# A ViT tower kernel: the decay column goes through device memory, block copies go to GpSimd, and several banks change hands

## The reference

```python
q, k = l2norm(silu(conv(x Wq))), l2norm(silu(conv(x Wk)));  v = silu(conv(x Wv))
alpha, beta = sigmoid(x Wa), sigmoid(x Wb)
def step(St, inp):                       # a scan over the 3137 tokens
    Sk = St @ kt
    Sn = a * (St - b * Sk[:, None] * kt[None, :]) + b * vt[:, None] * kt[None, :]
    return Sn, Sn @ qt
out = linear(zc_rmsnorm(gdn) * silu(x Wg), Wo)
```

## Time and profile before

| | |
|---|---|
| median of 3 runs | 950.95 us (950.13 to 955.2) |
| the profiled execution: time, span | 952.8 us, 951.1 us |
| PE busy | 866.4 us (91%) |
| DVE busy | 672.8 us (71%) |
| ACT busy | 515.1 us (54%) |
| POOL busy | 323.4 us (34%) |
| DMA | 42.52 MB, mean 45 GB/s |

### The profile page before, as it was taken

How to read it: one execution, slowest core, us unless ns; L and a number is a source line. 1 busy time by engine, 2 the same in 40 slices (tenths; PEclk the granted TensorE clock), 3 DMA queues, 4 the chain that set the end, 5 groups by cost and what they waited for, 6 DMA issues and landing times. The chain is left out here.

```text
span 951.1 us, 31438 instructions
## 1 busy us (share of the span) xinstructions
PE 866.4 (91%) x11991; PEld 656.8 (69%) x11991; DVE 672.8 (71%) x2445; ACT 515.1 (54%) x1846; POOL 323.4 (34%) x430
## 2 busy tenths in 40 slices
PE   4799999999999999999999999999977699999996
PEld 2467777777777777777776777777666477777675
DVE  4466778777778777777878777777773486777534
ACT  0445555556655565665555565655543346566664
POOL 3112222122222212222222222222210048889875
PEclk9989999999999999999999999999996699999999
DMA  2000111111111000000000000000000214334341
GB/s 53 6 7 7 51 40 51 40 51 46 30 51 41 29 21 26 28 26 29 29 18 29 18 29 26 28 29 13 24 25 12 89 45 122 112 106 128 101 117 56
DMA packets 60160, 42.52 MB, mean 45 GB/s; under 512 B 3233, under 2 KB 52579, under 8 KB 60012
## 3 DMA queue, kind: packets, MB, share of 16 engines
q1 hardware_dynamic: 59163, 39.98, 14.0%
q10 hardware_dynamic: 848, 0.54, 0.2%
HBM read 20.97 MB, written 19.53 MB: 43 GB/s over the span
## 5 line engine op out<-in xcount | busy, mean ns | idle before, releaser
L408 ACT ACTIVATE logit<-bank 128x2 f32<-128x2 f32 x100 | 17.4, 174 | 161.0 <-PE bank L1010 161.0
L1009 PE MATMUL bank<-SA,work 128*128 128x386 f32 x200 | 94.9, 558 | 3.5 <-ACT work L511 2.9
L1500 ACT ACTIVATE work<-bank,b1mix 128x512 f32<-128x512 f32 x96 | 66.0, 687 | 58.2 <-PE bank L1592 58.1
L1618 PEld LDWEIGHTS bank<-work 128*128 128x128 f32 x768 | 89.5, 192 | 11.5 <-issue 11.5
L1618 PE MATMUL bank<-work 128*128 128x128 f32 x768 | 89.6, 275 | 0.0
L1592 PE MATMUL bank<-work 128*128 128x512 f32 x192 | 86.5, 593 | 0.0
L592 POOL TENSOR_TENSOR expo<-euler,logit 128x8 f32<-128x8 f32 x25 | 40.9, 1638 | 133.0 <-ACT logit L408 133.0
L1010 PE MATMUL bank<-SB,work 128*128 128x256 f32 x200 | 61.2, 388 | 0.0
L612 POOL TENSOR_TENSOR oscale<-ovar,half_neg 128x4 f32<-128x4 f32 x25 | 25.2, 1008 | 105.3 <-DVE ovar L854 105.3
L716 DVE TENSOR_TENSOR work<-bank,work 128x128 f32<-128x128 f32 x100 | 29.2, 292 | 44.5 <-PE bank L997 42.7
L1010 PEld LDWEIGHTS bank<-SB,work 128*128 128x128 f32 x200 | 39.5, 197 | 28.6 <-issue 3.1
(11 more groups left out here) (239 smaller groups left out, 2339.9 us busy)
## 6 DMA issues: line engine op xcount, KB each, us to landing
hn_kept<-work SPq DMA_DIRECT2D x25, 256.0 KB, 2.3
hnT_kept<-work SPq DMA_DIRECT2D x25, 256.0 KB, 2.3
work<-hnT_kept SPq DMA_DIRECT2D x25, 256.0 KB, 3.1
work<-hn_kept SPq DMA_DIRECT2D x25, 256.0 KB, 3.3
out_dram<-work SPq DMA_DIRECT2D x24, 256.0 KB, 2.5
tv<-in_L_ffn_tv_W_dram SPq DMA_DIRECT2D x16, 256.0 KB
work<-in_x_dram SPq DMA_DIRECT2D x23, 102.0 KB
work<-in_projections_dram ACTq DMA_DIRECT2D x1, 257.0 KB
```

What stands on the lines that cost most here:

```text
L1009: mm(t[:, 0:386], xs[p][:, b, HIST:XW], SA[:, 0:386], start=True, stop=False)
L1500: ins = nc.scalar.activation(hid[f][:, :], ps[:, :], ACT.Relu, bias=b1mix[:, of[0], f:f + 1])
L1618: ins = mm(by4(bank[2 + par])[:, t, :], hid[f][:, t * C:(t + 1) * C], w2T[of[t]][:, f, :], start=(f == 0 and t == 0), stop=(f == FB - 1), ...
```

## The change

Seven edits. (1) `g`: row 0 of `decay` and `glast` now lie in one tile `decay_g`; SP writes that row to device memory and, when it has landed, reads it back as a column (128x4 single elements) and as a broadcast row. The five small PE operations go. (2) The six copies of `Xd` and `Yd` blocks move from ACT to POOL. (3) `level_blocks(6)` writes bank 7 and no longer waits for `X`'s level-5 blocks, only for `Y`'s. (4) The transposed `rmat` goes to bank 2 and stands before `level_blocks(6)` on PE; it waits for the decay scan. (5) `og` is transposed into bank 7, and `wo` moves into the next iteration, behind `km`. (6) POOL computes `expo` after `rmat`. (7) DVE takes the E statistics one level earlier, and `expo1`, `ab` and `kd` before `new_blocks(4)`; on ACT the relu comes after the copies of `X`'s last block and `ogT`.

```diff
@@ SP, at the end of an iteration
+                if on(j, LF):
+                    s = j + LF
+                    sp.wait_ge(glast_ready, s + 1)
+                    sp.dma_start(g_dram[s:s + 1, :], decay_g[0:1, :]).then_inc(g_out, 16)
+                    sp.wait_ge(g_out, 16 * (s + 1))
+                    need(sp, gs_ready, s - 1)
+                    need(sp, state_ready, s - 1)
+                    sp.dma_start(g_raw[s % 2][:, 0:NB], g_dram[s, 0:NB * C].rearrange("(b t) -> t b", b=NB), ...).then_inc(g_in[s % 2], 16)
+                    sp.dma_start(g_raw[s % 2][:, NB:3 * NB], g_dram[s, NB * C:NB * C + 2 * NB].partition_broadcast(D)).then_inc(g_in[s % 2], 16)
@@ ACT
-                    act.wait_ge(Y_ready, 5 * (s + 1))
-                    for r in (0, 1):
-                        nc.scalar.copy(Y[sub(r), :, sub(r)], Yd[par][sub(r)])
-                    for r in (2, 3, 0, 1):
-                        nc.scalar.copy(X[par][sub(r), :, sub(r)], Xd[par][sub(r)])
...
-                (the relu of gf, L488 to L495)
...
-                    nc.scalar.copy(ogT, by4(bank[5])).then_inc(ogT_ready, 1)
+                    nc.scalar.copy(ogT, by4(bank[7])).then_inc(ogT_ready, 1)
+                (the relu of gf)
@@ POOL: the block of expo moves behind that of rmat, and then
+                if on(j, LI):
+                    s = j + LI
+                    pool.wait_ge(Y_ready, 5 * (s + 1))
+                    for r in (0, 1):
+                        ins = nc.gpsimd.tensor_copy(Y[sub(r), :, sub(r)], Yd[par][sub(r)])
+                    ins.then_inc(Yd_kept, 1)
+                    for r in (2, 3, 0, 1):
+                        ins = nc.gpsimd.tensor_copy(X[par][sub(r), :, sub(r)], Xd[par][sub(r)])
+                    ins.then_inc(Xd_kept, 1)
+                    pool.wait_ge(Xd_kept, s + 1)
@@ DVE
-                    dve.wait_ge(g_ps, s + 1)
+                    dve.wait_ge(g_in[par], 32 * (s // 2 + 1))
-                    nc.vector.tensor_copy(gs[par][:, 4:12], small_ps[:, 20:28]).then_inc(alpha0_kept, 1)
-                    dve.wait_ge(alpha0_kept, s + 1)
-                    nc.vector.tensor_tensor(gs[par][:, 0:4], small_ps[:, 16:20], gs[par][:, 8:12], ALU.mult).then_inc(gs_ready, 1)
+                    nc.vector.tensor_tensor(gs[par][:, :], g_raw[par][:, 0:NB], g_raw[par][:, 2 * NB:3 * NB], ALU.mult).then_inc(gs_ready, 1)
@@ DVE: the order from level 2 to level 4
before: grow(2), kd, vmean, vt, new_blocks(3), hn, grow(3), E statistics, new_blocks(4), expo1/ab/ab0, grow(4)
after:  grow(2), E statistics, new_blocks(3), hn, grow(3), expo1/ab/ab0, kd, new_blocks(4), vmean, vt, grow(4)
@@ PE, level_blocks(6)
-                        pe.wait_ge(X5_ready, s0 + 1)
+                        pe.wait_ge(Yd_kept, s0 + 1)
+                        pe.wait_ge(Y5_ready, s0 + 1)
@@ PE, start of an iteration, behind km
+                if H_:
+                    pe.wait_ge(ogT_ready, h + 1)
+                    need(pe, hnT_ready, h)
+                    need(pe, o_ready, h + 1)
+                    (wo into bank 6)
@@ PE, before level_blocks(6)
+                if E_:
+                    pe.wait_ge(rmat_ready, 2 * (e + 1))
+                    if F_:
+                        pe.wait_ge(decay_ready, s1 + 1)
+                    (transpose of rmat into bank 2)
@@ PE, end of an iteration
-                (the transpose of rmat into bank 1, waiting for h0_kept, relu_ready and ssq_ready)
-                    for b in range(NB):
-                        tr(small_ps[:, 16 + b:17 + b], decay[0:1, b, :], ident[0:1, 0:1])
-                    mm(small_ps[:, 20:28], ones[0:1, :], glast[:, :], start=True, stop=True).then_inc(g_ps, 1)
-                (wo into bank 6)
```

More of the change, by code:

```diff
@@ L126, in vit_tower @@
         qT = [tile(NB * D, NB, D) for _ in range(2)]
-        decay = tile(NB * C, NB, C)
+        decay_g = tile(NB * C + 2 * NB)
+        decay = decay_g[:, 0:NB * C].rearrange("p (b c) -> p b c", b=NB)
+        glast = decay_g[0:1, NB * C:NB * C + 2 * NB]
         cdecay = tile(NB * C, NB, C)
@@ L175, in vit_tower @@
         qn2e = [sb(f"qn2e{i}", [D, NB]) for i in range(2)]
-        glast = sb("glast", [1, 2 * NB])
-        gs = [sb(f"gs{i}", [D, 12]) for i in range(2)]
+        gs = [sb(f"gs{i}", [D, NB]) for i in range(2)]
+        g_raw = [sb(f"g_raw{i}", [D, 3 * NB]) for i in range(2)]
         so2 = sb("so2", [D, NB])
@@ L816, in body @@
                     ins.then_inc(mv1_ready, 1)
-                new_blocks(4)
+                new_blocks(3)
+                if on(j, LH):
+                    s = j + LH
+                    h = h1buf[:, :, bass.ds(s, 1), :].rearrange("p b s c -> p b (s c)")
+                    dve.wait_ge(mv2_ready, s + 1)
+                    dve.wait_ge(rstd2_ready, s + 1)
+                    need(dve, hnT_ps, s)
+                    need(dve, hn_out, 16 * s)
+                    for b in range(NB):
+                        ins = nc.vector.tensor_scalar(hn[:, b, :], h[:, b, :], mv2[:, b, 0:1], rstd2[:, b:b + 1],
+                                                      ALU.subtract, ALU.mult)
+                    ins.then_inc(hn_ready, 1)
+                grow(3)
                 if on(j, LF):
@@ L975, in level_blocks @@
                         else:
-                            ins = mm(by64(blk_ps)[64:128, b], Bm[par][0:64, b, 64:128], Y[0:64, b, :], start=True, stop=True)
+                            ins = mm(by64(bank[7])[64:128, b], Bm[par][0:64, b, 64:128], Y[0:64, b, :], start=True, stop=True)
                     ins.then_inc(blk_ps_done, 1)
@@ L1017, in body @@
                     ins.then_inc(km_ps, 1)
+                if H_:
+                    pe.wait_ge(ogT_ready, h + 1)
+                    need(pe, hnT_ready, h)
+                    need(pe, o_ready, h + 1)
+                    for b in range(NB):
+                        ins = mm(by4(bank[6])[:, b, :], ogT[:, b, :], Wo_T[:, :], start=True, stop=True)
+                    ins.then_inc(wo_ps, 1)
                 level_blocks(1)
@@ L1107, in body @@
                     ins.then_inc(kq_ps, 1)
+                if isinstance(j, int) and j == first:
+                    fold_weights()
+                if E_:
+                    pe.wait_ge(rmat_ready, 2 * (e + 1))
+                    if F_:
+                        pe.wait_ge(decay_ready, s1 + 1)
+                    for b in range(NB):
+                        ins = tr(by4(bank[2])[0:KX, b, :], rmat[:, b, :], ident[:, :])
+                    ins.then_inc(rb_ps, 1)
                 level_blocks(6)
@@ L1115, in body @@
                 if C_:
-                    pe.wait_ge(state_ready, c + 1)
+                    need(pe, ogT_ready, c)
+                    if I_:
+                        pe.wait_ge(blk_ready, 6 * (s0 + 1))
                     for b in range(NB):
                         pe.wait_ge(og_ready, NB * c + b + 1)
-                        ins = tr(by4(bank[5])[:, b, :], og[:, b, :], ident[:, :])
+                        ins = tr(by4(bank[7])[:, b, :], og[:, b, :], ident[:, :])
                     ins.then_inc(ogT_ps, 1)
[L1121 to L1139, removed]
-                        tr(small_ps[:, 16 + b:17 + b], decay[0:1, b, :], ident[0:1, 0:1])
-                    mm(small_ps[:, 20:28], ones[0:1, :], glast[:, :], start=True, stop=True).then_inc(g_ps, 1)
-                if C_:
-                    pe.wait_ge(ogT_ready, c + 1)
-                    need(pe, hnT_ready, h + 1)
-                    pe.wait_ge(o_ready, c + 1)
-                    for b in range(NB):
-                        ins = mm(by4(bank[6])[:, b, :], ogT[:, b, :], Wo_T[:, :], start=True, stop=True)
-                    ins.then_inc(wo_ps, 1)
             iterations(body)
```

110 lines of the change are left out of this document (54 added, 56 removed).

## The result

The changed kernel takes 919.76 us (median of 4 runs, 915.49 to 923.53) against 951.12 for the kernel before on the same occasions: a ratio of 0.966, 95% interval 0.960 to 0.972. The profiled execution has a span of 915.1 us in 916.87 us, that of before 951.1 in 952.8.

A forecast was written before the change was run, and what follows sets the result against it. PE's list, in order, was taken to set the pace; 2.18 us removed less new waits of 0.69 and 0.45 gives a 26.4 us period, 28 us saved with start and tail: 923 us, range 900 to 938.

The forecast's parts named there:

- The work taken off PE: PE per iteration: `g` products 0.56 us, gap before L976 1.06, gap before L1132 0.56; together 2.18 of 27.53 us.
- B to K: From L976's start (B) to first projection (K): chain through DVE's `xs` takes 5.96 us, new wait 0.69.
- K to B: From first projection (K) to L976 (B): 20.42 us, with 0.45 us wait at level 4 update behind `expo`.
- What was costed at nothing: POOL's six copies (1.8 us), `wo` behind `km`, the moved L1132 and the trip of `g` (about 6 us) all hide.
- 10.4 after `glast`: The trip of `g` decides the period from 10.4 us after `glast` is ready, at K (first projection) + 29.
- Rival D: The trip of `g` takes more than its cover, so DVE's gs waits: slower, 967 us; chance 0.08.
- Rival B: PE's new waits do not show: 52 us gained, 899 us; chance 0.14.
- Rival C: Moved `expo` eats the gain: wait at level 4 1.5 us instead of 0.45, 947 us; chance 0.09.
- Rival E: PE's clock stays 1.00 in the steady stretch; in the tail the low stretch can move some us; no chance given.
- The sum: Whole run: 22 steps x 1.1 = 24.2 us, plus the tail, minus 0.5 at the start; total 28 us saved.
- The start: Iterations j = -1 and 0: the trip of `g` has less cover, minus 0.5 us.
- The end: Iterations j = 23 to 26, with fewer stages: some 1.5 us gained for j = 23, 2.5 for j = 24, 0.5 after.

The follow-up runs named there:

- the kernel with both waits removed: The kernel after with POOL's `expo` ahead of `rmat` again and DVE's `xs` ahead of level 6's block: 893.37 us, measured again 891.08 us.
- the expo run: The kernel after with POOL's block of `expo` put back ahead of `rmat`: 908.58 us, ratio 0.955.
- the runs with five and seven writes: The kernel after with the row of `g` written five or seven times, each waited for, before it is read: 922.98 us and 978.09 us.
- The kernel with three writes: The kernel after with the row of `g` written three times, each waited for, before it is read: 919.26 us, ratio 0.964.

## Why the prediction was right

923 us were predicted, 919.8 measured.

**The work taken off PE.** Right. The two gaps of the earlier trace rows are gone, the first by the copies alone (period 26.42), and the `g` products by the trip alone (27.00, 0.53 less than before where 0.56 was counted). That the relu was what held the second gap was argued from ACT's rows; no run moves it alone. Without any wait the prediction's sum gave 25.35, and the kernel with both waits removed has 25.15.

**B to K, 5.96 us.** Right in place and size. Level 6's block to the first projection is 442.11 - 436.16 = 5.95 us in the trace after; the prediction had put it together from five rows of before. The wait was 0.77 where 0.69 was expected, since PE's own way was a little shorter. That the chain is the cause was shown by moving `xs`.

**K to B, 20.42 us.** 462.45 - 442.11 = 20.34. The wait at level 4 is 0.40 (0.45 expected), and the expo run shows its cause. `expo` ended at 454.05, K + 11.94, as worked out.

**What was costed at nothing.** The copies on POOL took 1.89 us (1.8 expected) and nobody waits for them. `wo` behind `km` and the transpose of `rmat` have no wait. The trip took 5.1 us (460.89 to 466.0) against some 6, inside the bounds, and has 4 us to spare; the runs with five and seven writes bracket the point where it decides, at a trip between some 4.5 and 6.8 us longer, 9.6 to 11.9 us in all. The prediction's 10.4 after `glast` lies there. Rival D's mechanism is real; its transfer was simply short enough.

**Rival B** (no new waits, 899) fell: PE has two new waits. **Rival C** (the moved `expo` eats the gain) had the right place and about a quarter of the price, 0.40 us of wait for 1.5. **Rival E:** see below.

**The sum.** Between the first projections of j = 2 and j = 23 lie 578.1 us before (97.9 to 676.04) and 652.43 - 100.31 = 552.1 after: 26.0 saved in 21 steps, 1.24 each where 1.1 was predicted, or 23.1. The other two terms were mis-sized, in opposite directions. The start lost 2.4 us (the first projection of j = 2 at 100.31 instead of 97.9). The prediction took off 0.5 for it and counted 1.1 for the step of j = 1, which lies in this stretch: a gain of 0.6. The loss is not the trip's (gs does not wait in j = 0): in j = 0 there is no output stage to lie over the wait, and `expo` is late by itself. PE and DVE in j = 0:

```profile
62.26 0.65 PE L1018 MATMUL bank<-work 32*32 32x32 f32 x32 [2.28 <-DVE work L726]
```

```profile
60.52 0.17 DVE L820 TENSOR_SCALAR expo<-expo 128x8 f32<-128x8 f32 x1 [2.13 <-POOL expo L616]
```

With expo first the projection of j = 2 is back at 97.88. The end gave 12.4 us in the profiled execution (951.1 - 676.04 = 275.1 against 915.1 - 652.43 = 262.7), not 4.5. The traces put most of that surplus on PE's clock. The run with five writes has the same 26.29 us period and reaches j = 23 at 652.65, but needs 269.8 us from there, 7.1 more; 0.9 of it is a PE wait behind its longer trip. PE's windows of the same stretch, first in the kernel after, then in the run with five writes (length, busy, clock, DMA share, GB/s):

```profile
680.00:700.00 20.00, 14.13 (x282) 1.00 0.10 29
```

```profile
680.00:700.00 20.00, 16.75 (x281) 0.51 0.10 29
```

As many matrix instructions at the full clock of 2.4 GHz in one, at about half (0.51, its level of 1.2) in the other. In both, PE had been waiting for DVE and ACT in the iterations with fewer stages. The kernel before had the low clock there too, 0.67 in the iteration of j = 24. The mean clocks of the kernel after's four runs fall into pairs with their times: 0.989 and 0.983 with 915.5 and 916.9, 0.975 with 922.7 and 923.5. The kernel with three writes splits in the same way (0.989 with 915.7 and 916.5, 0.976 with 922.1 and 923.3). So the median of 919.8 lies between two cases 7 us apart: the slower is 28 us under the kernel before, the faster 35. What decides between them in a run was not tried, and only the faster case of the kernel after has a trace. That the slower one meets the predicted 28 us so closely, and the median the predicted 923 within 3.2, is in part luck: the steady steps saved some 3 us more than forecast, and the start came out 3 us worse.

What the prediction did not ask is whether the trip bought anything. In the kernel after it did not: with the products back on PE the time is the same, since the new wait covers them. It pays where no such wait stands: alone (0.53 us a step), with the copies (26.42 to 25.89), or with both waits removed (0.40).

## What to carry to other kernels

When several edits are made to an engine that sets the pace, write out for each of its waits the chain on the other engines that ends there and how much it has to spare; once PE's list is shorter than such a chain, further work taken off PE is worth nothing (here the trip), and the chain's own order is what pays: 1.1 us a step came from moving one product into a gap of its engine, and one POOL operation ahead of another. Time an edit alone as well as in the bundle: here two edits of seven were worth more without the other five. And place an operation that others wait for by who waits soonest, also for the first iterations, where less lies over a late one.

## What the runs showed of the hardware

A read of 512 single elements of 4 bytes from device memory (the column of `g`, 128 partitions by 4) lands 2.0 to 2.2 us after its issue, no later than the 2.3 us of 256 KB in 512 pieces; the broadcast of 32 bytes to 128 partitions behind it takes 2.6 to 3.1. The Trainium skill ("DMA: Bandwidth & Descriptors", Rules for kernel authors) says that a non-contiguous last dimension becomes one descriptor per element; at 512 elements these runs show no price for it. A row of 2 KB written to device memory and waited for takes 1.13 to 1.15 us when no large transfer goes just ahead of it (the repeated writes, and in the kernel after the first iterations, 41.76 to 42.91), and 1.88 us when it is issued 0.4 us behind 256 KB on the same queue. The Trainium skill ("DMA: Bandwidth & Descriptors", Anatomy of one DMA) gives a fixed cost of about 2 us, fitted to transfers issued from GpSimd; these went through SP's queue, where the short one is well under it.

Six GpSimd copies of 32 partitions by 128 elements took 0.3 us each, as on ScalarE before. The VectorE operations beside them kept their lengths: 0.65, 0.59 and 1.22 us (L854, L723, L862), and 0.65, 0.59 and 1.22 in the kernel before, where no copy ran on GpSimd.

PE's granted clock differed between executions of one program at the end of the kernel, and between steps of one execution where PE waits in each of them: the same projection took 0.92 us at the full clock and 1.58 in a step with a mean of 0.94.
